# Two-layer graph network on one core: W's loads on ScalarE's queue, and a new order of all queues

## What is computed

```
h = relu(layernorm(x))
A = adj + I;  L = A scaled by rowsum(A)^-1/2 on both sides
x = x + L @ (h @ W + b)                            # layer 0
h = relu(layernorm(x))
H = (adj != 0);  w = first row of adj
conv(h, W) = Dn * (H @ (Be * (H^T @ (h @ W^T))))   # Dn = 1/(H @ w), Be = 1/colsum(H)
g = layernorm(relu(conv(h, W1) + b1)) * gamma + beta
x = x + conv(g, W2) + b2 + h                       # layer 1
```

## Time and profile before

| what | us |
|---|---|
| median of 3 runs | 1919.46 (1917.72 to 1922.2) |
| the profiled execution's own time | 1921.86 |
| its span, first to last instruction | 1920.0 |
| granted clock over the span | 0.995 |

### The profile page before, as it was taken

How to read it: one execution, slowest core, us unless ns; L and a number is a source line. 1 busy time by engine, 2 the same in 40 slices (tenths; PEclk the granted TensorE clock), 3 DMA queues, 4 the chain that set the end, 5 groups by cost and what they waited for, 6 DMA issues and landing times.

```text
span 1920.0 us, 37001 instructions
## 1 busy us (share of the span) xinstructions
PE 1871.1 (97%) x9926; PEld 896.1 (47%) x9926; DVE 1663.5 (87%) x3177; ACT 1451.3 (76%) x2726; POOL 1226.8 (64%) x1554
## 2 busy tenths in 40 slices
PE   5889999999999999999999999999999999999998
PEld 2344444444444444444444444444444444444443
DVE  6998988988988988989988988988889988888774
ACT  5788778778778778778778778778778778787664
POOL 4766766756766666666766766766666766576660
PEclk9899999999999999999999999999999999999999
DMA  8254554554554554453554554554554554544333
GB/s 230 56 102 93 110 112 89 108 110 92 106 113 91 107 111 92 109 112 91 108 112 91 108 109 94 108 112 92 108 111 92 109 108 95 110 93 98 83 67 78
DMA packets 518735, 197.64 MB, mean 103 GB/s; under 512 B 466816, under 2 KB 483328, under 8 KB 518528
## 3 DMA queue, kind: packets, MB, share of 16 engines
q1 hardware_dynamic: 518528, 195.27, 47.6%
HBM read 48.31 MB, written 33.55 MB: 43 GB/s over the span
## 4 chain that ended last, share of the span: by engine, by line
PE 77%; issue 7%; DVE 6%; POOL 4%; DMA 3%; SPq 1%; ACT 1%; DVEq 0%; POOLq 0%; ACTq 0%
PE ps_u L405 28%; PE ps_e L405 14%; PE ps_x L416 14%; PE ps_z L416 7%; PE ps_y L416 3%; DMA raw_t<-bet_wide 2%; PE ps_y L456 1%; PE ps_y L458 1%; PE ps_y L457 1%; PE ps_t L393 1%; PE ps_t L395 1%; PE ps_t L394 1%; PE ps_e L456 1%; PE ps_e L458 1%; PE ps_e L457 1%
## 5 line engine op out<-in xcount | busy, mean ns | idle before, releaser
L405 PE MATMUL ps_u<-w2h,raw_t 128*128 128x512 f16 x2016 | 477.8, 380 | 0.0
L1488 POOL TENSOR_TENSOR base<-b_all,xh 128x512 f32<-128x512 f32 x128 | 210.4, 1644 | 366.3 <-DVE raw_w L1123 356.3
L405 PEld LDWEIGHTS ps_u<-w2h,raw_t 128*128 128x128 f16 x2016 | 195.0, 98 | 225.2 <-issue 2.8
L1065 DVE SCALAR_TENSOR_TENSOR raw_w<-ps_x,dn,b_all 128x512 f32<-128x512 f32 x192 | 141.8, 739 | 117.5 <-PE ps_x L416 117.0
L405 PE MATMUL ps_u<-w2l,raw_t 128*128 128x512 f16 x1008 | 238.1, 379 | 0.0
L770 ACT ACTIVATE bet_wide<-raw_w 128x1024 f16<-128x1024 f32 x128 | 134.2, 1048 | 77.3 <-DMA raw_t<-bet_wide 73.5
L1480 POOL TENSOR_TENSOR b_all<-x,b_all 128x512 f32<-128x512 f32 x128 | 166.9, 1304 | 15.5 <-DMA b_all<-in_b_dram 6.4
L1493 POOL TENSOR_TENSOR base<-base,raw_w 128x512 f32<-128x512 f32 x128 | 166.8, 1303 | 8.0
L1538 POOL TENSOR_SCALAR u<-ssq 128x2 f32<-128x2 f32 x64 | 31.7, 496 | 216.4 <-ACT raw_w L755 215.8
L1109 DVE TENSOR_TENSOR bet_wide<-raw_w,bet_wide 128x1024 f16<-128x1024 f32 x128 | 158.9, 1242 | 8.0 <-DMA raw_t<-bet_wide 4.3
L761 ACT ACTIVATE raw_w<-raw_w,nm,sc 128x1024 f32<-128x1024 f32 x128 | 151.9, 1232 | 18.4 <-POOL nm L1564 18.2
(11 more groups left out here) (174 smaller groups left out, 4860.7 us busy)
## 6 DMA issues: line engine op xcount, KB each, us to landing
x_t<-in_x_dram SPq DMA_DIRECT2D x128, 256.0 KB, 2.9
out_dram<-raw_w SPq DMA_DIRECT2D x128, 256.0 KB, 2.5
adj_t<-in_adj_dram SPq DMA_DIRECT2D x64, 128.0 KB, 2.1
raw_t<-bet_wide SPq DMA_TRANSPOSE x256, 3.3
raw_w<-in_W1T_dram SPq DMA_DIRECT2D x4, 512.0 KB, 6.6
h0T_hi<-h_hi SPq DMA_TRANSPOSE x128, 2.5
h0T_lo<-h_lo SPq DMA_TRANSPOSE x128, 2.4
raw_w<-in_W2T_dram SPq DMA_DIRECT2D x8, 256.0 KB, 4.9
```

The source lines that it names most:

```text
L405: mm = pe.matmul(ps, t[:, j * 128:(j + 1) * 128], w[:, j, :], start=(n == 0 and j == 0), stop=(n == 2 and j == blocks - 1))
L1065: return dve.scalar_tensor_tensor(out=z, in0=bank[:, :], scalar=dn1[:, p % 2, j:j + 1], in1=z if row is None else row[:, cols], op0=ALU.mu ...
L1488: pool.tensor_tensor(base[:, g % 6, :], x1b[:, :], xh[:, g % 2, :], ALU.add).then_inc(s_scr2, 1)
```

## The change

W's four loads are issued by ACT, as its first instructions (load_first_weight), and no longer by SP. All six orders are written anew.

- Head, SP: x of graphs 2 and 3 goes ahead of the first transpose; W1's loads go ahead of the second transpose; six of W2's eight blocks go ahead of the first transposes of h0.
- Head, TensorE: gram_of_weight(1), weight_sum(1) and six of eight blocks of beta_row stand before Y0(0); P(0) stands after Y0(1); T1(0) and T1(1) stand after Z0(3).
- The written-out head is longer: the loop runs from k = 6 and holds Y0 and Z0 of 2k+7 and 2k+8, one pair further ahead. P is of pair k+3 in place of k+2.
- Within the loop the items stand in another order on every queue; the number of instructions an engine runs is the same, but for the four loads.
- End: the same items in another order; among them M4(NP-1) goes ahead of Y2(NG-5), and SP's transpose trh(NG-1) ahead of the store st(NG-3).

The core of the diff (the orders of the long end and of the later head are left out):

```diff
@@ -32,7 +32,7 @@
     KI, KH = DIN // 128, DH // 128
     NP = NG // 2
     HK = KI // 2
-    STEADY_FROM, STEADY_TO = 4, NP - 16
+    STEADY_FROM, STEADY_TO = 6, NP - 16
     EARLY = 4
...
@@ -316,72 +316,74 @@
         sp.dma_start(out[g, :, :], out_t[:, g % 2, :]).then_inc(s_st[g % 2], 16)
 
     do_ldA(0); do_ldA(1); do_ldA(2)
-    load_weight(0, raw_w0, W, range(0, 4))
     load_edge_weights()
     do_ldX(0); do_ldX(1)
     load_row(b_all, b, s_b)
     load_gamma_beta()
-    do_trA(0); do_ldA(3); do_trA(1)
-    turn_edge_weights()
-    do_ldX(2); do_ldX(3); do_ldA(4)
+    do_ldA(3); do_ldX(2); do_ldX(3); do_trA(0)
     load_weight(1, raw_w1, W1T, range(0, 2))
     load_weight(1, raw_w1, W1T, range(2, 4))
-    do_trA(2); do_tr0h(0); do_tr0h(1); do_ldA(5); do_tr0l(0); do_tr0l(1); do_ldA(6)
+    turn_edge_weights()
+    do_ldA(4); do_trA(1)
     load_weight(2, raw_w2, W2T, range(0, 1))
+    load_row(b2_all, b2, s_rows)
     load_weight(2, raw_w2, W2T, range(1, 2))
     load_weight(2, raw_w2, W2T, range(2, 3))
     load_weight(2, raw_w2, W2T, range(3, 4))
-    load_row(b2_all, b2, s_rows)
     load_weight(2, raw_w2, W2T, range(4, 5))
     load_weight(2, raw_w2, W2T, range(5, 6))
+    do_tr0h(0); do_tr0h(1); do_ldA(5); do_trA(2); do_tr0l(0); do_tr0l(1)
     load_weight(2, raw_w2, W2T, range(6, 7))
     load_weight(2, raw_w2, W2T, range(7, 8))
     load_row(b1_all, b1, s_rows)
...
     for k in range(STEADY_FROM, STEADY_TO):
-        do_ldX(2 * k + 8); do_tr0h(2 * k + 6); do_tr0h(2 * k + 7); do_tr0l(2 * k + 6); do_tr0l(2 * k + 7)
-        do_trh(2 * k - 2); do_st(2 * k - 4); do_trl(2 * k - 2); do_trA(k+5); do_ldX(2 * k + 9)
-        do_trh(2 * k - 1); do_trl(2 * k - 1); do_st(2 * k - 3); do_ldA(k+10)
...
+        do_ldX(2 * k + 10); do_ldA(k+10); do_tr0h(2 * k + 8); do_tr0h(2 * k + 9); do_tr0l(2 * k + 8)
+        do_tr0l(2 * k + 9); do_trh(2 * k - 2); do_trl(2 * k - 2); do_st(2 * k - 4); do_trh(2 * k - 1)
+        do_st(2 * k - 3); do_ldX(2 * k + 11); do_trl(2 * k - 1); do_trA(k+6)
...
@@ -547,78 +549,81 @@
 
     gram_of_weight(0, raw_w0, range(0, 4))
     weight_sum(0, gram[:, 0, 0:N + 1])
-    do_P(0)
     gram_of_weight(1, raw_w1, range(0, 4))
-    do_Y0(0); do_Y0(1)
     weight_sum(1, gram[:, 1, 0:N])
-    do_Z0(0); do_P(1); do_Z0(1); do_Y0(2)
-    weight_sum(2, wsq[:, 0:KH])
-    do_Y0(3); do_Z0(2)
     beta_row(range(0, 2))
-    do_T1(0); do_Z0(3)
     beta_row(range(2, 4))
     beta_row(range(4, 6))
-    do_P(2); do_T1(1)
+    do_Y0(0); do_Y0(1); do_P(0)
+    weight_sum(2, wsq[:, 0:KH])
     beta_row(range(6, 8))
+    do_Z0(0); do_Z0(1); do_Y0(2); do_Y0(3); do_P(1); do_Z0(2); do_Z0(3); do_T1(0); do_T1(1); do_P(2)
...
     for k in range(STEADY_FROM, STEADY_TO):
-        do_M1(k); do_Y0(2 * k + 5); do_U(2 * k - 3); do_M6(k); do_Y2(2 * k - 4); do_P(k+2); do_T1(2 * k + 2)
-        do_M7(k); do_Z0(2 * k + 5); do_M5(k); do_Y0(2 * k + 6); do_Y2(2 * k - 3); do_M3(k); do_M4(k)
-        do_M2(k); do_T1(2 * k + 3); do_U(2 * k - 2); do_Z0(2 * k + 6)
...
+        do_M1(k); do_Y0(2 * k + 7); do_U(2 * k - 3); do_M6(k); do_Y2(2 * k - 4); do_T1(2 * k + 2); do_M7(k)
+        do_M5(k); do_Y2(2 * k - 3); do_Z0(2 * k + 7); do_M3(k); do_M2(k); do_Y0(2 * k + 8); do_M4(k)
+        do_P(k+3); do_T1(2 * k + 3); do_U(2 * k - 2); do_Z0(2 * k + 8)
...
@@ -774,146 +779,152 @@
         done(act, s_y2, g - 1)
         act.activation(uh[:, g % 2, :], u_bank(g)[:, :], ACT.Copy, scale=U_EVAC).then_inc(s_uh, 1)
 
-    do_rsum(0); do_rsum(1); do_rsum(2); do_A_hi(0); do_rsum(3); do_A_hi(1)
+    load_first_weight()
+    do_rsum(0); do_rsum(1); do_A_hi(0); do_rsum(2); do_rsum(3); do_A_hi(1)
     square_sum_b()
-    do_A_hi(2); do_rsum(4); do_rsum(5); do_cntH(0); do_cntH(1); do_rsum(6); do_rsum(7); do_h0_hi(0)
-    do_h0_hi(1); do_A_hi(3); do_h0(0); do_h0(1); do_cntH(2); do_cntH(3)
+    do_A_hi(2); do_h0_hi(0); do_h0_hi(1); do_rsum(4); do_rsum(5); do_h0(0); do_h0(1); do_cntH(0)
     split_hi(0, raw_w0, w0h, range(0, 1))
+    do_cntH(1)
     split_hi(0, raw_w0, w0h, range(1, 2))
     split_hi(0, raw_w0, w0h, range(2, 3))
-    do_P_hi(0); do_P_hi(1)
     split_hi(0, raw_w0, w0h, range(3, 4))
-    do_rsum(8); do_rsum(9); do_cntH(4); do_cntH(5); do_h0_hi(2); do_h0(2)
+    do_rsum(6); do_rsum(7); do_A_hi(3); do_cntH(2); do_cntH(3)
     square_sum_gamma(range(0, 1))
     square_sum_gamma(range(1, 2))
-    do_h0_hi(3); do_yh(0); do_h0(3)
     square_sum_gamma(range(2, 3))
     square_sum_gamma(range(3, 4))
-    do_yh(1)
     square_sum_gamma(range(4, 5))
     square_sum_gamma(range(5, 6))
+    do_h0_hi(2); do_h0_hi(3); do_h0(2); do_rsum(8); do_rsum(9); do_h0(3); do_A_hi(4)
     square_sum_gamma(range(6, 7))
...
+        do_sq(2 * k - 2); do_h0_hi(2 * k + 8); do_h0_hi(2 * k + 9); do_h0(2 * k + 8); do_h0(2 * k + 9)
+        do_sq(2 * k - 1); do_yh(2 * k + 7); do_thS(k); do_hn(2 * k - 2); do_hn(2 * k - 1)
+        do_hn_hi(2 * k - 2); do_uh(2 * k - 3); do_P_hi(2 * k + 4); do_tf(2 * k + 2); do_hn_hi(2 * k - 1)
+        do_P_hi(2 * k + 5); do_xh(2 * k + 4); do_xh(2 * k + 5); do_h(2 * k); do_yh(2 * k + 8)
+        do_vq(2 * k + 4); do_vq(2 * k + 5); do_tf(2 * k + 3); do_xh_hi(k+2); do_thA(k+1); do_h(2 * k + 1)
+        do_rsum(2 * k + 16); do_rsum(2 * k + 17); do_A_hi(k+8); do_cntH(2 * k + 10); do_cntH(2 * k + 11)
+        do_uh(2 * k - 2)
...
@@ -1207,208 +1218,216 @@
         done(dve, s_p, p - 1)
         dve.tensor_copy(HB[:, :, p % 2, :, N], WT[:, :, 2 * p:2 * p + 2]).then_inc(s_wr, 1)
 
...
+    do_Hu(0); do_ahat(0); do_dds(0); do_A_lo(0); do_Hu(1); do_ahat(1)
     split_edge_weights()
...
     gram_diagonal(0)
...
+    do_A_lo(1); do_bn0(0); do_ahat(2); do_aggr0(0); do_bn0(1)
     widen_beta()
...
+    do_aggr0(1); do_dds(1); do_u0(0); do_bn0(2)
     weight_magnitude(0)
...
+    do_aggr0(2); do_bn0(3); do_Hu(2); do_aggr0(3)
     weight_scale(0)
...
+    do_u0(1); do_A_lo(2); do_dds(2); do_ahat(3); do_h0_lo(0); do_h0_lo(1)
     split_lo(0, raw_w0, w0h, w0l, range(0, 1))
...
+    gram_diagonal(1)
     split_lo(0, raw_w0, w0h, w0l, range(1, 2))
...
+    weight_magnitude(1)
     split_lo(0, raw_w0, w0h, w0l, range(2, 3))
     split_lo(0, raw_w0, w0h, w0l, range(3, 4))
...
+    do_Hu(3); do_A_lo(3); do_Hu(4); do_w(0); do_w(1); do_cm(0); do_cm(1); do_ahat(4); do_inv(0); do_h0_lo(2)
+    do_HB_hi(0); do_HB_hi(1); do_inv(1); do_HB_lo(0); do_h0_lo(3); do_A_lo(4); do_yv(0); do_HB_hi(2)
+    do_HB_hi(3); do_HB_lo(1); do_HB_lo(2); do_HB_lo(3); do_ahat(5); do_yv(1); do_yl(0)
     weight_magnitude(2)
...
+    do_yl(1)
+    keep_beta_row()
+    do_x1(0); do_dm(0); do_w(2); do_P_lo(0); do_ri(0); do_x1(1); do_dn(0); do_cm(2); do_dds(3); do_st1(0)
+    do_st1(1); do_inv(2); do_aggr1(0); do_aggr1(1); do_HB_hi(4); do_HB_hi(5); do_yv(2); do_HB_lo(4)
+    do_bn0(4); do_HB_lo(5); do_yl(2); do_aggr0(4); do_yv(3); do_bn0(5); do_w(3); do_x1(2); do_aggr0(5)
+    do_st1(2); do_aggr1(2); do_dm(1); do_P_lo(1); do_ri(1); do_u0(2); do_yl(3); do_xh_lo(0); do_bn0(6)
+    do_x1(3); do_aggr0(6); do_A_lo(5); do_st1(3); do_Hu(5); do_cm(3); do_dds(4); do_ahat(6); do_inv(3)
+    do_aggr1(3); do_dn(1); do_HB_hi(6); do_HB_hi(7); do_HB_lo(6); do_HB_lo(7); do_Hu(6)
     weight_scale(1)
...
+    do_h0_lo(4); do_bn0(7); do_h0_lo(5); do_A_lo(6); do_aggr0(7); do_u0(3); do_ahat(7); do_w(4)
     split_lo_w1(range(0, 1))
     split_lo_w1(range(1, 2))
+    split_lo_w1(range(2, 3))
     do_yv(4)
...
     split_lo_w1(range(3, 4))
     split_lo_w1(range(4, 5))
...
+    do_tlA(0); do_h0_lo(6); do_tlS(0); do_yl(4); do_h0_lo(7); do_dds(5)
     split_lo_w1(range(5, 6))
...
     split_lo_w1(range(6, 7))
     do_x1(4); do_z1(0); do_xh_lo(1); do_z2(0); do_z5(0); do_cm(4); do_P_lo(2); do_bn0(8); do_yv(5)
...
+    do_aggr0(8); do_inv(4); do_dm(2); do_st1(4); do_z6(0); do_ri(2); do_yl(5); do_z3(0); do_HB_hi(8)
...
-        do_x1(2 * k + 4); do_ul(2 * k - 4); do_st1(2 * k + 4); do_z1(k); do_ahat(k+7); do_aggr1(2 * k + 4)
-        do_bn0(2 * k + 8); do_yv(2 * k + 5); do_aggr0(2 * k + 8); do_tlS(k); do_yl(2 * k + 5)
-        do_h0_lo(2 * k + 6); do_h0_lo(2 * k + 7); do_z6(k); do_out(2 * k - 4); do_hn_lo(2 * k - 2)
-        do_ul(2 * k - 3); do_x1(2 * k + 5); do_st1(2 * k + 5); do_z5(k); do_aggr1(2 * k + 5); do_z7(k)
-        do_w(k+4); do_cm(k+4); do_inv(k+4); do_HB_hi(2 * k + 8); do_HB_hi(2 * k + 9); do_hn_lo(2 * k - 1)
-        do_yv(2 * k + 6); do_HB_lo(2 * k + 8); do_out(2 * k - 3); do_z3(k); do_bn0(2 * k + 9); do_z4(k)
-        do_aggr0(2 * k + 9); do_dm(k+2); do_z2(k); do_u0(k+4); do_ri(k+2); do_P_lo(k+2); do_dn(k+2)
-        do_yl(2 * k + 6); do_xh_lo(k+2); do_tlA(k+1); do_A_lo(k+7); do_nmu(k); do_Hu(k+7); do_dds(k+6)
-        do_HB_lo(2 * k + 9)
...
+        do_x1(2 * k + 6); do_ul(2 * k - 4); do_Hu(k+7); do_z1(k); do_cm(k+4); do_dds(k+6); do_ahat(k+8)
+        do_inv(k+4); do_st1(2 * k + 6); do_HB_hi(2 * k + 8); do_HB_hi(2 * k + 9); do_h0_lo(2 * k + 8)
+        do_yv(2 * k + 7); do_bn0(2 * k + 10); do_h0_lo(2 * k + 9); do_aggr0(2 * k + 10); do_yl(2 * k + 7)
```

(12 more changed lines are left out.)

871 lines of the change are left out of this document (433 added, 438 removed).

## The result

The changed kernel takes 1927.02 us (median of 6 runs, 1925.54 to 1928.73) where the kernel before took 1920.62 in the same comparison (1917.72 to 1922.2): a ratio of 1.0037, with a 95% interval of 1.0027 to 1.0047. It is 6.4 us slower by the medians and 7 by the ratio. Forecast were 1913.0 us and a gain of 6.5; the time lies outside the range of 1905 to 1924. The profiled execution of the changed kernel has a span of 1926.5 us (before: 1920.0).

What follows compares the result with a forecast made beforehand. TensorE, busy 1871.1 of 1920.0 us, was taken as the bound, with DVE fuller in the head from 34.3 us. Gains of 3 + 1 + 2 + 0.5 = 6.5 us gave 1913.0 us, own range 1908 to 1917, overall 1905 to 1924.

Steps and rivals of the forecast that it cites:

- The 3 us of the head: Head up to about 75 us: x1(4), z1(0) and M1(0) come earlier; 3 us gained, bounds 0 and 4.7.
- W on ACT: Head: ACT issues W's loads; first matmul at about 4.2 us, b and what follows on SP up 1.9 us.
- W1 earlier: Head: W1's loads issued at 7.8 us, its gram ending by 18 to 19.5 instead of 24.9; POOL's sums move up too.
- beta_row ahead of Y0(0): Head, TensorE: six blocks run from about 20 to 27.5 us, where it waited or ran slowly; 4.7 us of TensorE's time.
- DVE holds the head: Rival, head: W1's and W2's gains end at a DVE 94% busy; gain 0 to 3 us, 1918 us, chance 0.25.
- 75 to 121 us: Rest of the head: an extra graph of layer 0 gives TensorE work where it waited; 1 us gained, bounds -2 and 3.
- The loop: Loop: the new order mostly removes Y0's waits for x1, two new tight places fit; 2 us gained, bounds 0 and 4.3.
- the rival of the falling loop: Rival, loop: Y2(2k-3) waits for a late ul, 0.3 us in some 48 periods, 14 us; 1929 us, chance 0.17.
- The end: End: last pair's chain starts 0.65 us earlier, last transpose not behind a store; 0.5 us gained, bounds -2 and 1.5.

Runs made afterwards that it cites:

- without the sums: Changed kernel with POOL's four weight_sums done on 64 of 512 columns and W1's quarters read from W1 itself, against the kernel before: 1.0017.
- the changed head with the order before behind it: Changed order up to about 58 us, the kernel before's order behind; here with POOL's sums on 64 of 512 columns: 0.9992 of before (full sums 1.0017).
- the two by two above: Changed head with full or one-eighth POOL sums, against the kernel before: order before behind 58 us 1.0017 and 0.9992, changed order behind 1.0037 and 1.0017.

## Why the prediction was wrong

Three steps failed. W1's earlier loads moved POOL's sums up, which was put at nothing and cost 4 to 5 us. The order from 75 us on was taken as a gain of 1 us, and its parts cost 6 us each in the kernel before. And the loop was to gain 2 us and lost about 2. The 3 us of the head did not come either.

*W on ACT.* Its mechanism was right (first gram at 3.85, forecast 4.2) and its worth is nothing: b, moved up by 1.9 us on the queue, landed 0.3 us sooner. The row on which that term rested was the time of issue, and the chain hangs on the landing. The rule of the Trainium skill, page "DMA: Bandwidth & Descriptors", section "Queues, rings and completion order", that the DMA engines take packets from the queues in turn, had the direction right: 1.2 us of the 1.9 were lost with the queue alone changed, where the estimate said up to 1, and 1.6 in the changed kernel.

*W1 earlier: the step that failed first.* The paragraph ended with "POOL's sums of W1's quarters move up with it", at no price. The price was 4 to 5 us. I had asked which queues the loads pass, and not what runs beside work that the loads release. The trace of before held the number: splits of W that took 2.61 us beside a sum.

*beta_row ahead of Y0(0).* Forecast from 20 to 27.5, found from 26.6 to 34.5; without the sums from 21.9 to 29.7. So about 5 of the 7 us are the sums, and the rest is a term that was mis-sized: six blocks began 1.9 us later than forecast and took 8.0 us and not 7.5. That TensorE gains the time that it used to wait did not hold even with small sums: in the changed kernel M1(0) then came at 67.0, 2 us sooner than before, and the time was still 1.0017; in the changed head with the order before behind it M1(0) came at 69.4, against 69.0 before, and the time was 0.9992 (0.9983 to 1.0001), where 3 us were claimed. The rival "DVE holds the head", a gain of 0 to 3 us, fits that last kernel. It doesn't fit the changed one: its sign, DVE full from 30 us on, is not there (5.9 us idle up to x1(4)), and it allows no loss.

*75 to 121 us.* I took a gain of 1 us with bounds of -2 and 3. The order from 58 to 153 us alone costs 6 us in the kernel before, and what is changed behind it, the extra pair included, as much. The step that failed is the sentence that the extra pair gives TensorE work where it waited: I wrote beside it that DVE has more of this work and did not follow it through. In that stretch DVE is the fuller engine, and the trace of the change from 58 to 90 us shows what follows: tlS(0) ahead of yl(4) on DVE, and both last splits of W1 between yl(4) and x1(4), made TensorE wait for both results. I looked at TensorE's order only.

*The loop.* The slacks came out thinner but held: Y2(2k-3) was to be in time by 0.57 us and is by 0.06, M3 by 0.35 and is by 0.35 (z5 ends at 931.61, M3 starts at 931.96), Y0(2k+8) by 0.9 and is by 0.79. The waits of Y0 for x1 between 200 and 1700 us fell from 3.7 to 0.2. But the 2 us did not come: over all the kernels' traces the new loop's period is 0.06 us longer. Part of the waits was chance in that one execution: the kernel with W on ACT and the same old loop has 1.3 us of them between 200 and 1400 us, and its ratio is 0.9994. The rest of the step that failed is that idle time was taken for the whole of what the loop can gain or lose: the new loop idles no more and takes longer for the same matmuls. The measured 1927 us lies in the range of the rival of the falling loop (1922 to 1936), and that is chance: the loop did not lose by waits for ul, and of the 14 us named for it some 2 are found. Slower came in the main from places that no rival named.

*The end.* Forecast 0.5; the idle time behind 1700 us fell by 0.7, the wait of the earlier trace rows went and the two waits of Y2 stayed at 2.9 us. No run tests it apart.

*What stays open.* What makes the new loop's period longer at equal idle time. In the two by two above the sums and the order behind the head add up. But the order from 58 to 153 us and what is changed behind it cost 6 us each alone and 6 together. That TensorE waits for the same late DVE in either case would explain it; it was argued and not tested.

## What to carry to other kernels

Before work is moved up, ask what it releases and what runs beside that: here a load that came 4 us sooner set off 2.5 us operations of GpSimd beside VectorE's critical chain, which cost 4 to 5 us. Where one engine is full, compare orders on that engine, step by step; an order that looks better on TensorE can be worse for what TensorE waits for. And read the landing of a transfer, not its issue, before counting a queue as a gain.

## What was not expected of the hardware

VectorE's operation on 128 x 2 values took 2.33 us beside a GpSimd operation of 2.60 us and 0.43 beside one of 0.69; it ended with GpSimd's in both. GpSimd's sums themselves took 2.34 to 2.62 us in both kernels, whether they held VectorE or not, so the harm shows on VectorE's side, as long operations and not as waits. TensorE ran at 1.2 GHz until 31.8 us with Y0(0) first and until 32.0 with beta_row first: whichever came first took about 2.6 us more and the other ran at full pace. The table's granted clock of 1.00 ahead of the trace's first record of the clock is no reading; the starts of the matmuls are.
